# Shared expert of the second routed layer: blocks of 512 tokens instead of 256, four result rows over two PSUM banks

## What is computed

```
shared = jax.nn.silu(xt @ sg_w.T) * (xt @ su_w.T) @ sd_w.T
...
y = jnp.einsum('tei,ehi->teh', h, wd)
routed = jnp.einsum('te,teh->th', w, y)
return (shared + routed).reshape(orig_shape)
```

```
x = x + jnp.tanh(g_ffn[1]) * _L1_ffn_ref(_layernorm(x, axis=-1), ...)
```

## Time and profile before

| | us |
|---|---|
| median of three runs | 1607.42 (1606.39 to 1613.87) |
| the profiled execution, its own time | 1603.92 |
| its span in the trace | 1602.1 |
| run 1 of the shared expert, from the first `CH` to the last `out` | 886.9 to 932.9 |
| run 2, from the first `CH` to the last statistics | 1145.9 to 1197.7 |

### The profile page before, as it was taken

One profiled execution on the slowest core, in us unless ns is written; L12 is line 12 of the kernel. 1 busy time (PEld: TensorE's weight loads), 2 busy tenths in 40 slices (PEclk: granted clock), 3 DMA queues, 4 the chain that ended last, 5 costly groups with the idle time before them and its releaser, 6 DMA issues. The chain is left out here.

```text
span 1602.1 us, 28284 instructions
## 1 busy us (share of the span) xinstructions
PE 1324.1 (83%) x9624; PEld 1110.0 (69%) x9642; DVE 1130.4 (71%) x2469; ACT 906.0 (57%) x1952; POOL 728.4 (45%) x753
## 2 busy tenths in 40 slices
PE   2689977899999999869974779899778965555898
PEld 0445555799999999735554779899776842345687
DVE  6447756688988988559966558778565649785654
ACT  3236652677877877457732447777426347464432
POOL 2223202367777777413321038888403930454444
PEclk8699997999999999889995789999899979676899
DMA  5000003456656656320014027676511000101000
GB/s 186 1 1 1 1 14 127 180 221 247 269 219 258 262 216 258 109 63 1 1 56 166 4 91 250 225 242 240 184 39 50 1 0 1 33 1 62 1 27 27
DMA packets 60780, 173.69 MB, mean 108 GB/s; under 512 B 10256, under 2 KB 42000, under 8 KB 51040
## 3 DMA queue, kind: packets, MB, share of 16 engines
q1 hardware_dynamic: 53152, 151.42, 26.4%
q0 software_dynamic: 7488, 20.46, 3.7%
HBM read 155.34 MB, written 16.52 MB: 107 GB/s over the span
## 5 line engine op out<-in xcount | busy, mean ns | idle before, releaser
L1812 POOL TENSOR_TENSOR l0m_e_DL<-l0m_e_DN,l0m_e_DH 128x256 fp32r<-128x256 f32 x192 | 183.4, 965 | 86.6 <-ACT l0m_e_DH L1655 85.5
L1720 DVE TENSOR_TENSOR l0m_e_UL<-l0m_e_U,l0m_e_UH 128x512 fp32r<-128x512 f32 x192 | 164.5, 862 | 10.7 <-ACT l0m_e_UH L1645 10.4
L1581 PE MATMUL PS<-l0m_e_CH,l0m_e_UH 128*128 128x256 f32 x480 | 138.5, 289 | 2.0 <-DVE l0m_e_CL L1755 2.0
L1581 PE MATMUL PS<-l0m_e_CH,l0m_e_UL 128*128 128x256 f32 x480 | 136.5, 284 | 0.0
L1581 PE MATMUL PS<-l0m_e_CL,l0m_e_UH 128*128 128x256 f32 x480 | 136.4, 284 | 0.0
L1645 ACT CAST l0m_e_UH<-l0m_e_U 128x512 fp32r<-128x512 f32 x192 | 118.1, 615 | 0.0
L1720 DVE TENSOR_TENSOR l1m_e_UL<-l1m_e_U,l1m_e_UH 128x512 fp32r<-128x512 f32 x96 | 85.5, 892 | 19.9 <-ACT l1m_e_UH L1645 19.2
L1812 POOL TENSOR_TENSOR l1m_e_DL<-l1m_e_DN,l1m_e_DH 128x256 fp32r<-128x256 f32 x96 | 85.2, 899 | 25.5 <-ACT l1m_e_DH L1655 24.4
L1581 PEld LDWEIGHTS PS<-l0m_e_CH,l0m_e_UH 128*128 128x128 f32 x480 | 92.8, 193 | 2.2 <-ACT l0m_e_UH L1645 2.2
L1581 PEld LDWEIGHTS PS<-l0m_e_CL,l0m_e_UH 128*128 128x128 f32 x480 | 92.9, 194 | 0.0
L1581 PEld LDWEIGHTS PS<-l0m_e_CH,l0m_e_UL 128*128 128x128 f32 x480 | 92.7, 193 | 0.0
(11 more groups left out here) (610 smaller groups left out, 4752.9 us busy)
## 6 DMA issues: line engine op xcount, KB each, us to landing
l0m_e_U<-in_l_up SPq DMA_DIRECT2D x24, 2048.0 KB
l0m_e_DN<-in_l_down SPq DMA_DIRECT2D x24, 1024.0 KB, 5.0
l1m_e_U<-in_l_up SPq DMA_DIRECT2D x24, 1024.0 KB, 6.4
l1m_e_DN<-in_l_down SPq DMA_DIRECT2D x24, 512.0 KB, 3.9
CTX<-in_ctx SPq DMA_DIRECT2D x2, 2048.0 KB, 10.4
l1a_GA<-results_by_choice SPq DMA_DIRECT2D x16, 256.0 KB, 6.0
l1m_c_GA<-results_by_choice SPq DMA_DIRECT2D x16, 256.0 KB, 4.7
Z<-in_l_b_rows SPq DMA_DIRECT2D x24, 128.0 KB
```

Of the source, the lines that this page charges most:

```text
L1581: ins = nc.tensor.matmul(hb(u)[:, a * SLOTS:(a + 1) * SLOTS], w[:, f % RING, k, a, :], x[:, t % 2, k, :], start=(p == 0), stop=(p == len(p ...
L1720: nc.vector.tensor_tensor(UL[:, f % RING, :, :, :], U[:, t % 2, :, :, f * P:(f + 1) * P], UH[:, f % RING, :, :, :].bitcast(F32), ALU.subtr ...
L1812: nc.gpsimd.tensor_tensor(DL[:, f % RING, :], DN[:, t % 2, f, :], DH[:, f % RING, :].bitcast(F32), ALU.subtract).then_inc(s_dl, 1)
```

## The change

The block becomes 512 tokens (`BANK`), so a run has two blocks of four units, and R is 4. Every up product has 512 columns, and ScalarE's and VectorE's instructions on `CH`, `CL`, `SG`, `HH`, `HL` are twice as long and half as many. The tile `HR` is gone: VectorE multiplies in place into `SG`, and so silu of unit u waits for `s_hl` of u-2 instead of `s_hr`. The four result rows of a block lie two to a bank in banks 6 and 7; TensorE waits for the pair of rows that was in the bank, and `out` waits for the pair to be finished. Products, passes and the number of down matmuls stay as they are.

```
-                NF, TOK = self.FF // P, 256
+                NF, TOK = self.FF // P, BANK
...
-                    HR = sb_in(c, f"{tag}_HR", [P, 2, TOK])
+                    HR = SG
...
-                    yb = lambda b: PS[:, 6 + b % 2, 0:D]
+                    yb = lambda b: PS[:, 6 + b // 2 % 2, b % 2 * D:(b % 2 + 1) * D]
...
-                                    if b >= 2:
-                                        pe.wait_ge(s_out, b - 1)
+                                    if b >= 4:
+                                        pe.wait_ge(s_out, b // 2 * 2 - 2)
...
-                                    act.wait_ge(s_hr, u - 1)
+                                    act.wait_ge(s_hl, u - 1)
...
-                                dve.wait_ge(s_y, b + 1)
+                                dve.wait_ge(s_y, b // 2 * 2 + 2)
```

## The result

The changed kernel took 1613.42 us (median of 19 runs), the kernel before, in as many runs beside it, 1605.35: a ratio of 1.0049, 95% interval 1.0034 to 1.0065. That is +7.9 us (+5.5 to +10.4); +7 was forecast. It is slower beyond its interval, and by less than the 0.5% that was called no difference.

What follows compares the result with a forecast made beforehand. Run 1 was taken as TensorE-bound; in run 2 TensorE waits on VectorE, which ends the run. Terms of +1.3 and +5.9 us gave +7.2, taken as +7: 1607.4 becomes 1614.4 us, range 1608 to 1620.

Steps and rivals of the forecast that it cites:

- The sum and the sign: Both runs of the shared expert together: slower, +1.3 us in run 1 and +5.9 in run 2, taken as +7.
- The tail of run 2: Behind run 2's last `out`: eight combinings left instead of two, +6.7 us; waiting for a pair of results adds +0.4.
- the rival that the tail is partly hidden: End of run 2: some combinings lie beside the last `down`; +4 us, 1611, within 0.5% but nearly even; chance 0.10.
- The three waits inside run 2: TensorE's stops for hidden values inside run 2, 0.74, 1.35 and 1.35 us, all go: -3.4 us.
- the rival of the chained units: The in-place product makes silu wait for `HL` of two units before, in each unit: +5 us more, 1619; chance 0.08.
- The wait before the last `down`: TensorE waits longer for VectorE before each run's last `down`: +0.95 us in run 1, +1.0 in run 2.
- The head: Start of each run: longer first `CH` and `CL` delay the first matmul, +0.7 us in run 1, +0.95 in run 2.
- Streaming: Up products: one of 512 columns takes 0.2325 us, a pair of 256 takes 0.24; -0.6 us a run.
- The clock: Last `down` of each run: unchanged in run 1, 0; 11 more slow matmuls in run 2, +1.0 us.
- the low clock lasts through the last `down` of each run: Rival, slower by over 0.5%: all 48 matmuls of each last `down` slow after longer gaps; +13.5 us, 1621; chance 0.22.
- Within 0.5%: Whole kernel: the change makes no difference the measurement can tell, under about 8 us; chance 0.59.
- slower: Whole kernel: the change costs over 0.5%, from +8 us; chance 0.38.

Runs made afterwards that it cites:

- e1: Against the kernel before: 512-token blocks in run 2 of the shared expert only, run 1 kept at 256; 1.0026, +4.2 us.
- e3: The changed kernel with run 2's combinings moved to where VectorE idles or nothing waits for it; 1.0010 of the kernel before, +1.6 us.
- e7: Against the kernel before: run 2 alone with 512-token blocks and its combinings moved, run 1 kept at 256; 0.9964, -5.8 us.
- e12: The kernel of e7 measured once more against the kernel before; 0.9971, -4.7 us.
- e2: Against the kernel before: 512-token blocks in run 1 of the shared expert only, run 2 kept at 256; 1.0044, +7.0 us.
- e10: The kernel of e2 measured a third time, beside an unchanged copy, against the kernel before; 1.0025, +4.0 us.
- e11: The kernel of e2 plus 11 filler matmuls ahead of run 1's last `down`; 1.0003 of the kernel before, +0.5 us.
- the three without fillers: Three measurements of one kernel, only run 1 at 512 tokens and no filler matmuls, against the kernel before; together 1.0031.

## Why the prediction was right, step by step

- **The sum and the sign** held: +7 forecast, +7.9 measured (5.5 to 10.4). That the sum came out so close is luck: its halves were wrong in opposite ways: run 2 was put at +5.9 and is +4.1 to +4.6 (traces) or +4.2 (e1); run 1 was put at +1.3 and is about +4 or more end to end (+7.0, +3.9, +4.0; +3.7 as the difference of the whole change and e1). The errors, -1.6 and some +3, offset each other.
- **The tail of run 2**, +6.7 us for six combinings and +0.4 for the pair: right. 9.5 us against 2.8 behind the last result. e3, e7 and e12 turn this term around; the rival that the tail is partly hidden fell with it.
- **The three waits inside run 2**, -3.4 us: right; none is left. Silu is released by TensorE in every unit, as forecast, so the rival of the chained units fell without an experiment.
- **The wait before the last `down`**: 4.94 in run 2 and 2.83 us in run 1, where 5.05 and 3.0 were worked out; +1.0 and +0.9 over before. Right.
- **The head**: from the first `CH` to the first matmul 2.45 us in run 2 (1.49 before, +0.96; +0.95 forecast) and 4.71 in run 1 (4.10, +0.6; +0.7 forecast).
- **Streaming** was mis-sized in run 2, and this is where 1.2 of its 1.8 us went (the clock, below, has the rest); TensorE's last matmul came 3.0 us earlier, counted from the run's start, where 1 was forecast. 512 columns start 0.227 us apart there, a unit takes 2.72 us (silu from 1163.80 to 1166.52) and not 2.79. By parts, from the first matmul to the last `down`: 42.45 us before, 35.27 after, 7.2 less. Of it 2.9 us are the 24 `down` matmuls that now come later, 3.4 the waits, and +1.0 the last wait; 1.9 us are left for streaming and gaps where -0.75 was put. In run 1 a unit took 2.80 us, as forecast. By the figure of the Trainium skill, "TensorE: Matmul & The Clock Gate", section "Wait — 56ns, not 53.3ns?", 2.5 ns over N / 2.4 GHz, a unit would be an estimated 2.59 us, which fits neither run.
- **The clock** failed as a term, in its place. In run 2 I put 11 more slow matmuls for the longer wait; the low stretch covered 20 against 16 before, +0.4 us instead of +1.0. In run 1 I put nothing, since both neighbouring waits had shown the same 3.4 us. The step that failed is that reading: one trace shows one outcome, and after a wait of 2.8 us several were possible (none slow in the changed kernel, 16 in e2 and e10, 28 in e3), and after the old 1.9 us too (16, or none in e12). Its size stays open: e11 against the three without fillers gives 4.5 us, with an interval of 0.5 to 8.5, while by the slow matmuls in the traces it is about nothing (12 on average against 13). The bounds (-1.5 to +3.0 on the +1.3, so up to +4.3) held two of the three measurements. The rival "the low clock lasts through the last `down` of each run" was seen in no trace (28 of 48 is the most); for run 1 the end-to-end times would fit it.

The range (1608 to 1620) held the 1613.42. Its low end had a slip: with all matmuls of the last `down` fast in both runs, run 2 gives back its 16 + 11 matmuls at 1.2 GHz, 2.5 us, and run 1 its 16, another 1.5, so 4.0 us and not 2.5; it should have been 1606 to 1607. "Within 0.5%" with 0.59 and "slower" with 0.38 are a fair picture of a result at 1.0049.

## What to carry to other kernels

When a loop does a piece of other work per round, halving the rounds moves the rest behind the loop: count what is left there, and put it where that engine idles instead; here this was worth 7 to 9 us of run 2 with 512 tokens and about 4 with 256, against the larger block's own gain of none. Work that is not needed for the last hand-over belongs behind it, not ahead. In these traces a wait of 1.9 to 4.9 us on TensorE ahead of a burst of matmuls was followed by anything from none to 28 slow matmuls, and one trace is one draw: price such a wait from both sides, and check it by filling it.

## What the runs showed of the hardware that I had not expected

The same up product of 512 columns, with the clock at 2.4 GHz, starts every 0.227 us in run 2 and every 0.233 us in run 1 of the same program. A unit has twelve of them, so it shows in ScalarE's silu, which starts when a unit is done. From the timeline of ACT after, run 1 and then run 2:

```profile
904.52 0.60 ACT L2064 ACTIVATE l1m_sh_SG<-PS 128x512 f32<-128x512 f32 x1 [1.70 <-PE PS L2034]
907.32 0.60 ACT L2064 ACTIVATE l1m_sh_SG<-PS 128x512 f32<-128x512 f32 x1 [1.70 <-PE PS L2034]
...
1163.80 0.60 ACT L2064 ACTIVATE l1m_sh_SG<-PS 128x512 f32<-128x512 f32 x1 [1.61 <-PE PS L2034]
1166.52 0.60 ACT L2064 ACTIVATE l1m_sh_SG<-PS 128x512 f32<-128x512 f32 x1 [1.61 <-PE PS L2034]
```

Units took 2.80 and 2.72 us in e3 as well (silu at 905.57 and 908.37, at 1162.49 and 1165.21), while with 256 columns they took 1.44 us in both runs of the kernel before. No experiment looked for the cause.

Unchanged code varied more than the change itself: the stages ahead of run 1 took 884.1 to 895.0 us in the traces of the changed kernel and the twelve experiments, and the experts' tiles 209.2 to 216.3. The mean granted clock of an execution goes with its time: of the changed kernel's, one of 1607.10 us had 0.911 and one of 1624.27 us 0.898. Only the stage's own length, and many runs end to end, told the kernels apart, and for run 1 the two gave different answers.
